# Graph network on one core: the destination order goes from pairs of chunks to single chunks

## The reference

```python
h = jnp.maximum(_layernorm(x, axis=-1), 0.0)
x = x + _L0_gnn_ref(h, edge_weight, edge_index)     # layer 0
h = jnp.maximum(_layernorm(x, axis=-1), 0.0)
x = x + _L1_gnn_ref(h, ..., edge_index)             # attention, 8 heads, then 1
# layer 0, with row, col = src, dst:
msg_fwd = w * x[col, :c_half]
x_fwd = segment_sum(msg_fwd, row, n) / clip(deg_row, 1)
msg_bwd = w * x[row, c_half:]
x_bwd = segment_sum(msg_bwd, col, n) / clip(deg_col, 1)
return concatenate([x_fwd, x_bwd], axis=-1)
```

## Time and profile before

| | us |
|---|---|
| median of 3 runs (3293.35 to 3298.26) | 3296.31 |
| profiled execution | 3294.2 |
| its span in the profile | 3292.4 |
| busy PE / DVE / ACT / POOL | 2243 / 1918 / 1739 / 1928 |
| first gather of order D | 962.6 |
| first gather of attention layer 1 | 1697.5 |

### The profile page before, as it was taken

The page is one execution under the profiler, slowest core; times in us unless marked ns, Lnnn a source line. Parts: engine busy times, 40 slices in busy tenths (PEclk is TensorE's granted clock), DMA queues, the critical chain, the costliest instruction groups (busy, mean ns, idle before and its releaser), DMA issues. The chain is left out here.

```text
span 3292.4 us, 46358 instructions
## 1 busy us (share of the span) xinstructions
PE 2243.2 (68%) x14916; PEld 1669.3 (51%) x14916; DVE 1917.8 (58%) x4213; ACT 1738.7 (53%) x5133; POOL 1928.0 (59%) x1999
## 2 busy tenths in 40 slices
PE   6887778677758877343577777777767566655653
PEld 4785667567747766233343333333335445444542
DVE  8985788577747776222446666666686233333336
ACT  3995677578747776222334444344438344444444
POOL 1006666666666666666635656665645566666664
PEclk8998999799878999555688888888888777777776
DMA  2011111111141112111545656665641333333335
GB/s 60 1 41 40 40 44 43 43 45 45 45 47 44 45 44 53 47 46 47 58 140 160 169 164 173 169 170 157 168 104 33 87 92 89 91 89 90 90 90 77
DMA packets 114882, 270.48 MB, mean 82 GB/s; under 512 B 34543, under 2 KB 51670, under 8 KB 114646
## 3 DMA queue, kind: packets, MB, share of 16 engines
q0 software_dynamic: 89088, 245.53, 30.5%
q1 hardware_dynamic: 25558, 21.98, 2.1%
HBM read 250.96 MB, written 16.42 MB: 81 GB/s over the span
## 5 line engine op out<-in xcount | busy, mean ns | idle before, releaser
L435 POOL DMA_INDIRECT rows_near<-table_a,s_idx_S x464 | 474.1, 1022 | 286.0 <-issue 115.4
L435 POOL DMA_INDIRECT given<-table,s_idx_S x464 | 449.2, 968 | 301.5 <-issue 126.8
L1166 DVE TENSOR_TENSOR work<-work,bank 128x129 f32 (+2 forms) x928 | 391.0, 421 | 362.4 <-remote 163.1
L435 POOL DMA_INDIRECT rows_near<-table,s_idx_S x464 | 446.8, 963 | 252.7 <-issue 127.8
L435 POOL DMA_INDIRECT rows_near<-table_b,s_idx_D x464 | 450.0, 970 | 230.9 <-issue 101.9
L950 PE MATMUL bank<-scratch,oh 128*128 128x512 f32 x928 | 488.1, 675 | 15.9 <-DVE scratch L1413 11.7
L818 PE MATMUL bank<-rows_near,oh 128*128 128x129 f32 x1856 | 331.0, 330 | 246.6 <-issue 179.5
L647 ACT ACTIVATE e_att<-lrelu 128x32 f32<-128x32 f32 (+1 forms) x232 | 49.9, 215 | 740.6 <-DVE lrelu L1402 490.0
L818 PEld LDWEIGHTS bank<-rows_near,oh 128*128 128x128 f32 x1856 | 289.0, 234 | 282.1 <-issue 232.8
L935 PE MATMUL bank<-sort_ring,scratch 128*128 x2784 | 154.0, 169 | 329.4 <-ACT scratch L643 285.2
L538 ACT ACTIVATE scratch<-scratch,given 128x128 f16<-128x128 bf16 x840 | 284.1, 388 | 170.8 <-DVE scratch L1130 146.7
(11 more groups left out here) (222 smaller groups left out, 4799.8 us busy)
## 6 DMA issues: line engine op xcount, KB each, us to landing
rows_near<-table_a,s_idx_S POOLq DMA_INDIRECT x464
rows_near<-table_b,s_idx_D POOLq DMA_INDIRECT x464
rows_near<-table,s_idx_S POOLq DMA_INDIRECT x464
given<-table,s_idx_S POOLq DMA_INDIRECT x464
table<-scratch SPq DMA_DIRECT2D x25, 260.0 KB
table<-scratch SPq DMA_DIRECT2D x25, 128.5 KB, 3.0
xs<-in_x SPq DMA_DIRECT2D x1, 3072.0 KB
out_x<-scratch SPq DMA_DIRECT2D x24, 128.0 KB, 1.7
```

The costliest lines, as they stand in the source:

```text
L435: nc.gpsimd.indirect_dma_start(out=to, out_offset=None, in_=table[:, :], in_offset=bass.IndirectOffsetOnAxis(ap=s_idx[order][:, c:c + 1], ...
L1166: v.tensor_add(a, a, psum).then_inc(sum_free[o], 1)
```

## The change

Order D is aligned to single chunks. Each tile begins on a multiple of 128 edges; the worst case is 440 chunks or 110 quads. Order S stays as it was. Each chunk of D has a sum of its own in a ring of nine, three in a bank. VectorE adds them with `add_chunks`, in step q up to `added_by(q)`, the next multiple of three above 4q, so that a bank's three sums go together: 3, 3 and 6 in turn. The tile numbers of D are now one per chunk, loaded every three steps. The second half of D is 216 chunks wide for 240.

The blocks are always two tiles (the last is one) and start at step `FIRST_D = 104`. A block's rows, its root and scales, and its normalisation stand in one step of VectorE and ScalarE; its transposes are in the next step of TensorE, its features, dense product and evacuation in the one after. TensorE does the transposes of a block before the dense product of the block ahead of it. The score products are written between the dense ones. The table of layer 1 has seven staging slots.

```diff
+CHUNKS_D = -(-((E + T * (P - 1)) // P) // QUAD) * QUAD
+ALIGN = {"S": GP * P, "D": P}
-SUMS0 = 6
+SUMS0 = {"S": 6, "D": 9}
+BLOCKS_D = [range(t, min(T, t + 2)) for t in range(0, T, 2)]
+def added_by(q):
+    return min(CHUNKS_D, -(-(QUAD * q + 1) // 3) * 3)
+STAGED = {"1": 7, "2": 4}
...
             def sum_rows(o, phase, q):
                 pe.wait_ge(oh_ready[o], q + 1)
+                gp = ALIGN[o] // P
                 for k in range(QUAD):
                     c = q * QUAD + k
-                    g, slot = c // GP, c % SLOTS
-                    if k == 0:
-                        pe.wait_ge(sum_free[o], g + QUAD // GP)
+                    g, slot = c // gp, c % SLOTS
+                    if c % (gp * SUMS0[o] // 3) == 0:
+                        pe.wait_ge(sum_free[o], g + SUMS0[o] // 3)
...
             def beside_rows(q):            # TensorE
-                n = q - FIRST - 4
-                if 0 <= n - 1 < len(BLOCKS):
-                    block_dense(n - 1)
-                if 0 <= n < len(BLOCKS):
-                    block_transposes(n)
+                n = q - FIRST_D - 1
+                if 0 <= n < len(BLOCKS_D):
+                    block_transposes(n)
+                if 0 <= n - 1 < len(BLOCKS_D):
+                    block_dense(n - 1)
...
+            def add_chunks(o, phase, q, tiles):
+                at, to = added_by(q - 1) if q else 0, added_by(q)
+                dve.wait_ge(chunks_summed, SLOTS + phase * CHUNKS + to)
+                for c in range(at, to):
+                    add_group(o, acc[o], tiles[c - at], c, sum0(o, c), SUMS0[o])
+            def layer0_chunks(o, phase, between):
+                one_hots(o, phase, 0)
+                for q in range(QUADS_D + 1):
+                    if q % 3 == 0:
+                        at, to = added_by(q - 1) if q else 0, added_by(q + 2)
+                        tiles = tile_numbers(mybir.EngineType.DVE, o, TILE_AT + at, to - at)
+                    if q + 1 < QUADS_D:
+                        one_hots(o, phase, q + 1)
+                    part, po, h, b = part_beside(phase, q)
+                    if b is not None:
+                        place_batch(part, po, h, b)
+                        if b == BATCHES - 1:
+                            merge(part, po, h)
+                    add_chunks(o, phase, q, tiles[(added_by(q - 1) if q else 0) - at:])
+                    between(q)
...
             def beside_rows(q):            # VectorE
-                n = q - FIRST - 2
+                n = q - FIRST_D
-                if 0 <= n - 4 < len(BLOCKS):
-                    for t in BLOCKS[n - 4]:
-                        dense("1", HD, HEADS, s_src1, tab_1, t)
-                if 0 <= n - 1 < len(BLOCKS):
-                    scales(n, BLOCKS[n - 1].start, BLOCKS[n - 1].stop)
-                if 0 <= n < len(BLOCKS):
-                    block_rows(n)
-            layer0("D", 1, beside_rows)
+                if 0 <= n < len(BLOCKS_D):
+                    block_rows(n)
+                    scales(1 + n, BLOCKS_D[n].start, BLOCKS_D[n].stop)
+                if 0 <= n - 2 < len(BLOCKS_D):
+                    for t in BLOCKS_D[n - 2]:
+                        dense("1", HD, HEADS, s_src1, t)
+            layer0_chunks("D", 1, beside_rows)
```

More of the change, by code:

```diff
@@ L60, with complete_at @@
 BLOCKS = [range(tiles_done(2 * q), tiles_done(2 * q + 2)) for q in range(FIRST, QUADS)]
-SUMS0 = 6
+SUMS0 = {"S": 6, "D": 9}
+BLOCKS_D = [range(t, min(T, t + 2)) for t in range(0, T, 2)]
+def complete_at(t):
+    return min(CHUNKS_D, (E + (t + 1) * (P - 1)) // P)
+def added_by(q):
+    return min(CHUNKS_D, -(-(QUAD * q + 1) // 3) * 3)
+FIRST_D = next(q for q in range(QUADS_D) if added_by(q) >= complete_at(BLOCKS_D[0].stop - 1))
+assert all(added_by(FIRST_D + n) >= complete_at(b.stop - 1) for n, b in enumerate(BLOCKS_D)) and FIRST_D + 2 < QUADS_D
+STAGED = {"1": 7, "2": 4}
 COUNTED_AT = (T + 1) // 2 + 1
 RANK_AT = COUNTED_AT + 3
-assert RANK_AT + T < CUT[1] // QUAD - 4
+assert RANK_AT + T < CUT["S"][1] // QUAD - 4
 HEAD_EARLY = 2
@@ L70 @@
 assert CHUNKS % SLOTS == 0 and CHUNKS <= 512 and P * COLS >= E and FULL < P and COLS % BATCH == 0
-assert SLOT_W <= 12 * HD and T % BLOCK == 0 and all(c % 2 == 0 for c in CUT)
+assert SLOT_W <= 12 * HD and T % BLOCK == 0 and all(c % 2 == 0 for o in "SD" for c in CUT[o])
 def build(nc, x, src, dst, edge_weight, W_heads, b_heads, a_heads, g_heads, beta_heads,
@@ L364, in part_beside, with landings_before @@
         def part_beside(phase, step):
-            if phase == 0 and step >= CUT[1] // QUAD:
-                return 2, "D", 0, batch_after(step - CUT[1] // QUAD)
+            if phase == 0 and step >= CUT["S"][1] // QUAD:
+                return 2, "D", 0, batch_after(step - CUT["S"][1] // QUAD)
             return (1, "S", 1, batch_after(step)) if phase == 0 else (3, "D", 1, batch_after(step))
+        def landings_before(phase, slot):
+            return sum((length - slot + SLOTS - 1) // SLOTS for length in (CHUNKS, CHUNKS_D, CHUNKS)[0:phase])
         def tile_numbers(engine, o, at, n):
@@ L607, in _ @@
                         beside_rows(q)
-            for q in range(QUADS, QUADS + 5):
+            for q in range(QUADS_D, FIRST_D + len(BLOCKS_D) + 2):
                 beside_rows(q)
@@ L880, in _ @@
                     if b is not None:
-                        place(part, h, b)
+                        place(part, po, h, b)
                     if phase:
                         beside_rows(q)
-            for q in range(QUADS, QUADS + 5):
+            for q in range(QUADS_D, FIRST_D + len(BLOCKS_D) + 2):
                 beside_rows(q)
```

159 lines of the change are left out of this document (81 added, 78 removed).

## The result

The changed kernel took 3343.63 us (median of 4 runs, 3342.11 to 3352.36), the kernel before 3294.83 us (4 runs): a ratio of 1.0161, 95% interval 1.0147 to 1.0174. Between the medians that is 49 us, by the ratio 53 (48 to 57); the forecast was 3338 us. The profiled execution has a span of 3342.0 us against 3292.4.

The account below looks back on a forecast made before the run. TensorE was taken to set the pace beside the sort, with batches, not gathers, the limit. Fewer gathers +1, place of the add +50, quiet stretch 0, blocks -7 gave +44 on 3294.2: 3338 us, range 3284 to 3378 (own range 3312 to 3370).

Parts of the forecast that it names:

- the loop with its allowance: Sort stretch: VectorE, ScalarE, TensorE loop of 332 us plus 32 for stalls and slow clock, 365 against 315.
- The place of the add: Sort stretch: adding the step's own quad ahead of the next batch makes a new wait, +50 us (0 to +82).
- the ring-slot waits vanish: Sign in the sort: VectorE's waits for a slot of the sort's ring, 57 us in all, disappear.
- more than 345: Sign in the sort: first to last batch of the last sort part takes more than 345 us.
- VectorE's waits at the adds: Sign in the sort: VectorE's adds wait for TensorE's sums for 60 us or more, 14 before.
- ScalarE's waits for VectorE: Sign in the sort: ScalarE's scalings wait for VectorE more than before; no size given.
- stalls on the path: Sort stretch: half of 65 us of TensorE stalls and slow clock taken as lying on the loop, 32 us.
- 24 fewer gathers: End of order D: removed gathers lie beside the blocks and save nothing; first block starts later, +1.4 us.
- The blocks: Finishing node tiles up to layer 1's first gather: 98 us against 104.9, -7 us (-22 to +8).
- The standstills: Blocks: VectorE's 15.3 us standstill was kept in the sum, with full DMA engines and empty chunks reading row 0.
- rival 2: Sort stretch: TensorE's idle gaps drop its clock to 1.2 GHz, +96 us, 3384 us; chance 0.12.
- rivals 1 and 3: Sort: TensorE still sets the pace, 3275 us (chance 0.20); or the loop bites little, +15, 3303 us (0.13).

Follow-up runs that it names:

- e10: e4 with order D's tile numbers back at places where no load after the first begins on a multiple of four: 3276.16 us, ratio 0.9961.
- e1: Changed kernel with order D's tile numbers stored three places further on, so each load of twelve begins on a multiple of four: 3308.52 us, ratio 1.0050.
- e11: e4 with order D padded to 464 chunks again, its second half 240 wide for 216: 3295.27 us, ratio 1.0003.
- e4: e1 with adds two quads late, ahead of the batch, while the sort runs, and a ring of 12 sums there: 3276.93 us, ratio 0.9963.
- e5: Kernel before with only the new order of the blocks and the seven staging slots: 3287.39 us, ratio 0.9987.
- e6: e4 with order D's places without an edge holding their lane as row number instead of 0: 3280.06 us, ratio 0.9964.
- e7: e6 with the same row numbers for places without an edge in order S too: 3285.63 us, ratio 0.9975.
- e9: e4 with five unread TensorE products behind each chunk's product between sort and blocks (the quiet stretch): 3285.85 us, ratio 0.9988.

## Why the prediction came out right, and what was wrong in it

The forecast of 3338 us (own range 3312 to 3370) met 3343.6, and the direction rested on the right mechanism. That it came so near is in part luck: the loop with its allowance was put too long, the loads were left out, and the two made up for each other.

1. *The place of the add, right.* "A new wait, and what is queued behind it is what ScalarE and then TensorE wait for": put two quads back, the kernel is 66 us faster (e10). The signs named came, but for one threshold: the ring-slot waits vanish, and the stretch is 362 us where "more than 345" was asked, but VectorE's waits at the adds are 55 us (14 before) where 60 had been asked for. ScalarE's waits for VectorE ahead of the sort's scalings grew only if the unnamed ones are read too: by name they are 68 us before and 65 changed, but with those that the profile calls "issue" they go from 82 to 142, and each of the 19 "issue" waits of over 0.3 us ends 0.03 to 0.04 us after VectorE's first one-hots of that batch.
2. *The loop's length, too long with its allowance.* The forecast's 332 us and its 32 for "stalls on the path" are for 52 steps, and stand against 315 before; from the first batch (step 1) to the last (step 51) are 50. e1, which has the loop without the slow loads, took 332.7 for these, 346 for 52. So loop and allowance were +49 in the forecast and are +31 here. One piece of the loop is shown wrong: it had TensorE's sums of the whole quad (1.06) and then 1.1 us of handover. The adds need one to three of the quad's chunks, and start 0.15 us after the product that they wait for (median of 22 such waits in the changed kernel's trace), in 15 of the 22 cases 0.55 or 0.77 us after the quad's first product. So the loop by itself is shorter than was worked out, and more of e1's 346 us is stalls; no run separates the two.
3. *The loads, overlooked.* This is the step that failed: a term that the sum did not have. 2.5 us before 17 quads, 29 us of the stretch and 36 of the whole (e1). The prediction gave the loads of tile numbers no price, though their rows were there: in the kernel before, loads of eight took 0.60 us in order D, and the attention layers' loads of eight, which begin two places off a multiple of four, 1.84 (the two rows of line 372 above). The Trainium skill ("Runtime: NRT & Kernel Launch", section "Instruction fetch mechanics") gives some 200 ns for each register loaded; the page tells of loads from HBM, and here the numbers lie in SBUF. This case comes near it where the start is not a multiple of four numbers (12 in 2.73, 8 in 1.84: 0.23 each), and not where it is (12 in 0.85). An estimate from that page's figure alone is 2.4 us for 12 numbers.
4. *24 fewer gathers, mis-sized.* Put at +1.4 us and nothing saved; measured 13 us saved (e11 against e4), in the blocks. It is not the gathers' own time: in e11 the last gather of order D leaves at 1648.1, and the blocks go on to 1680.7. What went away beside the last blocks is the quad's one-hots, adds and sums; which of these costs the time no run shows.
5. *The blocks, right in sign.* -7 forecast, -4 (-9 to 0) in e5. The six blocks without sums took 30 us (31 forecast), the end 14.4 (15). The six with sums took 46 us, not 37: two of the slow loads (some 2 us: the six take 43.8 in e1), and waits for TensorE.
6. *The standstills.* One of 15.3 us was left among the blocks. The changed kernel has seven of 10.2 to 15.0 us, all ahead of the blocks; the kernel before has two ahead of them (11.3 and 16.5) and the one of 15.3 among them, so the -5 us from first to last block in the table owes as much to where a standstill fell. The reading that full DMA engines and the row of the empty chunks cause them found no support in e6 and e7, and e9, where TensorE has more to do in the quiet stretch, has none there.
7. *The clock* (rival 2) fell from 0.94 to 0.82 over the stretch and is 0.85 in e1, 0.90 in e10 and 0.92 in e4, so it fell with the idle time and came back with the slack. TensorE's busy time in the stretch is 241.5 us in the changed kernel and 231.5 in e10, with the same products: up to 10 of the 66 us may be the clock's. No run separates them. The lower level for the whole stretch, as rival 2 had it, did not come.

Of the others, rivals 1 and 3 are refuted by the 60 us in the stretch.

In ratios: the new order of the blocks -0.1%, 24 fewer chunks -0.4%, the place of the adds +2.0% with these loads. Without the last, and with the larger ring, the changes of the diff make a kernel that is 0.4% faster than the one before (e4, e10).

## What to carry to other kernels

When an instruction is moved, ask first what stands behind its wait on the same engine: an add of 0.29 us, moved from "two quads late, ahead of the batch" to "own quad, behind it", put a whole engine into a loop, and from then on slow loads on that engine cost time that had been free. An experiment that brings only the slack back (e10) tells this apart from one that makes the work itself cheaper (e1): both gave time back, and only together do they say where the cause lies. A slow load costs nothing behind instructions that are already issued, and nearly its full time behind a chain of instructions that wait for one another, so look at what stands ahead of it. And look at short instructions that read a table by an offset: a count or a start that changes can change their duration several times over.

## What the runs showed of the hardware

- A load of numbers from SBUF into an engine's registers: 0.60 us for 8 and 0.85 us for 12 when it begins on a multiple of four numbers (16 bytes, counted from the tile's start), 1.84 us for 8 and 2.73 us for 12 when not. Four numbers more cost 0.25 us in the first case, each number 0.23 in the second; 14 from a multiple of four took 1.31 us (e4). Starts of 0 and of 4 modulo 8 are alike (e1).
- Such a load holds back what VectorE gets after it, not what it has got before it: 2.5 us of idle time before each of 17 one-hots behind adds (changed kernel), none at 12 of 13 places behind `place_batch` (e10), with loads of 2.73 us in both.
- In the 18 us that hold the gathers of the 12 empty chunks the DMA engines were busy for 0.69 of the time at 41 GB/s where all 128 lanes read one row, and for 0.15 at 44 GB/s where they read 128 rows (e4, e6). The kernel took the same time.
- TensorE busy for 65% of the quiet stretch, with products that nobody reads, had a granted clock of 0.75; without them it was busy for 40% and had 0.54. VectorE's standstills of over 10 us went, and nothing went faster (e9, e4).
